# A transformer block in one queue order: a new order of the steps on every engine, and the modulation products in pieces

## The reference

```python
ada = silu(c) @ W_ada + b_ada
shift_msa, scale_msa, gate_msa, shift_mlp, scale_mlp, gate_mlp = split(ada, 6)
h = layernorm(x) * (1 + scale_msa) + shift_msa
x = x + gate_msa * attention(h)          # 16 heads of 18 columns, full softmax
h = layernorm(x) * (1 + scale_mlp) + shift_mlp
x = x + gate_mlp * (gelu(h @ W_fc1 + b_fc1) @ W_fc2 + b_fc2)   # 1152 hidden columns
```

## Time and profile before

| | us |
|---|---|
| three runs | 1205.43, 1207.51, 1208.17 |
| median | 1207.51 |
| the profiled execution's own time | 1206.03 |
| its span, first to last instruction | 1204.2 |
| PE busy | 1161.6 (96%) |
| DVE, ACT, POOL busy | 922.7, 858.0, 578.6 |
| granted TensorE clock, mean of the span | 0.982 |

### The profile page before, as it was taken

The page is one execution under the profiler, slowest core; times in us unless marked ns, Lnnn a source line. Parts: engine busy times, 40 slices in busy tenths (PEclk is TensorE's granted clock), DMA queues, the critical chain, the costliest instruction groups (busy, mean ns, idle before and its releaser), DMA issues.

```text
span 1204.2 us, 28774 instructions
## 1 busy us (share of the span) xinstructions
PE 1161.6 (96%) x10375; PEld 996.8 (83%) x10375; DVE 922.7 (77%) x1928; ACT 858.0 (71%) x1485; POOL 578.6 (48%) x619
## 2 busy tenths in 40 slices
PE   6888999999999999999999999999999999999987
PEld 5656888888888888888888888888888888888777
DVE  5578878878878788787778888877888887877553
ACT  4378777777777777777777787777777777778721
POOL 3012444555544445554454555445455544544664
PEclk9679999999999999999999999999999999999999
DMA  9455554455545445554544555555445555444220
GB/s 283 127 173 159 159 152 154 155 175 172 165 152 174 140 148 173 173 165 156 168 148 150 163 177 169 161 159 165 144 149 177 175 160 158 153 150 161 81 68 20
DMA packets 133815, 186.94 MB, mean 155 GB/s; under 512 B 24284, under 2 KB 102150, under 8 KB 133675
## 3 DMA queue, kind: packets, MB, share of 16 engines
q1 hardware_dynamic: 129193, 175.81, 46.8%
q10 hardware_dynamic: 4482, 9.29, 2.6%
HBM read 119.92 MB, written 64.60 MB: 153 GB/s over the span
## 4 chain that ended last, share of the span: by engine, by line
PE 85%; SPq 5%; DMA 4%; DVE 2%; issue 1%; ACT 1%; POOL 1%; ACTq 0%; POOLq 0%; DVEq 0%
PE a_bank L851 11%; PE x_bank L764 11%; PE turn_bank L818 9%; PE b_bank L851 8%; PE score_bank L789 7%; PE b_bank L865 6%; PE st_bank L806 6%; PE b_bank L866 6%; PE b_bank L867 6%; PE a_bank L832 4%; PE x_bank L772 4%; DMA o_rows<-on 2%; PE x_bank L738 2%; PE a_bank L738 1%; SPq L609 1%
## 5 line engine op out<-in xcount | busy, mean ns | idle before, releaser
L1128 DVE TENSOR_REDUCE mx<-score_bank 128x2 f32<-128x512 f32 x512 | 332.5, 685 | 93.2 <-PE score_bank L789 91.3
L938 ACT ACTIVATE e<-st_bank 128x1024 f32<-128x1024 f32 x256 | 262.6, 1026 | 162.7 <-PE st_bank L806 162.1
L1285 POOL TENSOR_TENSOR gl<-gl_raw,gh 128x512 fp32r<-128x512 f32 (+1 forms) x160 | 197.0, 1239 | 181.2 <-DVE gh L1193 181.2
L931 ACT CAST ql<-mxt 4x256 fp32r<-4x256 f32 x512 | 205.6, 402 | 5.3
L865 PE MATMUL b_bank<-w,gh 128*128 128x288 f32 x576 | 179.2, 311 | 2.0 <-DVE tmp L1199 1.9
L866 PE MATMUL b_bank<-w,gh 128*128 128x288 f32 x576 | 170.7, 296 | 0.0
L867 PE MATMUL b_bank<-w,gl 128*128 128x288 f32 x576 | 169.7, 295 | 0.0
L818 PE MATMUL turn_bank<-e,ve 128*32 128x256 f32 x2048 | 125.5, 386 | 0.4 <-ACT e L938 0.4
L806 PE MATMUL st_bank<-ql,kl 58*128 58x256 f32 x1024 | 118.0, 309 | 6.6 <-ACT e L938 5.9
L789 PE MATMUL score_bank<-kl,ql 58*128 58x256 f32 x1024 | 120.9, 315 | 3.1 <-DVE mx L1128 1.7
L851 PE MATMUL a_bank<-xh,w 128*128 128x256 f32 x640 | 111.7, 297 | 4.3 <-DVE xr L1107 2.8
(11 more groups left out here) (152 smaller groups left out, 2497.6 us busy)
## 6 DMA issues: line engine op xcount, KB each, us to landing
qk_rows<-qst SPq DMA_DIRECT2D x128, 256.0 KB, 3.7
ql<-qk_rows SPq DMA_DIRECT2D x384, 72.0 KB
kl<-qk_rows SPq DMA_DIRECT2D x378, 72.0 KB
o_rows<-on SPq DMA_DIRECT2D x128, 128.0 KB
gate<-gates SPq DMA_DIRECT2D x32, 432.0 KB, 4.6
x<-in_x SPq DMA_DIRECT2D x32, 288.0 KB, 4.1
out<-x SPq DMA_DIRECT2D x32, 288.0 KB, 2.2
xin<-in_x ACTq DMA_DIRECT2D x30, 288.0 KB, 6.4
```

The lines of the kernel that those rows point to most:

```text
L931: last = nc.scalar.copy(rows[:, :, :, a, :], src)
L938: nc.scalar.activation(e[:, j % 4, :, :, :].rearrange("p i u l -> p (i u l)"), st_bank[:, :, :, :].rearrange("p i u l -> p (i u l)"), ACT. ...
L1128: nc.vector.tensor_reduce(mx[:, j // HP, i, :, col:col + 1], score_bank[i][:, :].rearrange("p (t l) -> p t l", t=NT), AX.X, ALU.max).then_ ...
L1285: nc.gpsimd.tensor_tensor(gl[:, cols], g[:, cols], gh[:, cols].bitcast(F32), ALU.subtract).then_inc(g_lo, 1)
```

## The change

All fifteen lists are new; the steps in a period are the same 40 on TensorE, 29 on ScalarE, 45 on VectorE, 17 on GpSimd and 51 on SP. The order of TensorE's period:

```diff
 PE_ORDER = [
-    ("fc2", -3, 0), ("proj", -2, 0), ("st", 0, 1), ("s", 0, 6), ("xt", 2, 0), ("proj", -2, 1), ("st", 0, 2),
-    ("s", 0, 7), ("xt", 2, 1), ("fc2", -3, 1), ("st", 0, 3), ("fc2", -3, 2), ("pv", 0, 0), ("qk", 2, 0),
-    ("fc2", -3, 3), ("s", 1, 0), ("st", 0, 4), ("lt", -2, 0), ("fc2", -3, 4), ("s", 1, 1), ("st", 0, 5),
-    ("lt", -2, 1), ("qk", 2, 1), ("fc2", -3, 5), ("s", 1, 2), ("st", 0, 6), ("fc1", -2, 0), ("s", 1, 3),
-    ("st", 0, 7), ("qk", 2, 2), ("fc1", -2, 1), ("s", 1, 4), ("pv", 0, 1), ("fc1", -2, 2), ("v", 2, 0),
-    ("fc1", -2, 3), ("st", 1, 0), ("s", 1, 5), ("fc1", -2, 4), ("v", 2, 1),
+    ("fc1", -3, 0), ("st", 0, 3), ("s", 1, 0), ("xt", 2, 1), ("fc1", -3, 1), ("pv", 0, 0), ("fc1", -3, 2),
+    ("qk", 2, 0), ("fc1", -3, 3), ("fc1", -3, 4), ("s", 1, 1), ("st", 0, 4), ("qk", 2, 1), ("proj", -2, 0),
+    ("s", 1, 2), ("st", 0, 5), ("fc2", -3, 0), ("proj", -2, 1), ("s", 1, 3), ("st", 0, 6), ("fc2", -3, 1),
+    ("st", 0, 7), ("s", 1, 4), ("fc2", -3, 2), ("qk", 2, 2), ("pv", 0, 1), ("s", 1, 5), ("st", 1, 0), ("lt", -2, 0),
+    ("fc2", -3, 3), ("v", 2, 0), ("st", 1, 1), ("s", 1, 6), ("lt", -2, 1), ("fc2", -3, 4), ("v", 2, 1),
+    ("fc2", -3, 5), ("st", 1, 2), ("s", 1, 7), ("xt", 3, 0),
 ]
```

ScalarE's period, in which the five gelu steps (`fc1`) stand between the exponentials `st` 3 and 4, and `mb(1,0)` behind `st(0,7)`:

```diff
 ACT_ORDER = [
...
-    ("lt", -2, 1), ("st", 0, 5), ("qk", 2, 1), ("st", 0, 6), ("st", 0, 7), ("fc1", -2, 0), ("oh", -1, 0),
-    ("fc1", -2, 1),
+    ("v", 1, 0), ("lt", -3, 1), ("st", 0, 1), ("v", 1, 1), ("oh", -2, 0), ("st", 0, 2), ("xt", 2, 0), ("st", 0, 3),
+    ("fc1", -3, 0), ("xt", 2, 1), ("fetch", 4, 0), ("fc1", -3, 1), ("mb", 0, 1), ("fc1", -3, 2), ("qk", 2, 0),
+    ("oh", -2, 1), ("fc1", -3, 3), ("fc1", -3, 4), ("st", 0, 4), ("pv", 0, 0), ("qk", 2, 1), ("st", 0, 5),
+    ("st", 0, 6), ("st", 0, 7), ("mb", 1, 0), ("qk", 2, 2), ("pv", 0, 1), ("st", 1, 0), ("lt", -2, 0),
 ]
```

TensorE's head, its first lines. It ends with `("st", 3, 2), ("s", 3, 7), ("xt", 5, 0)` where the old one ended with `("fc1", 0, 4), ("st", 3, 0), ("s", 3, 5), ("v", 4, 1)`; the new one has no `fc1`, the new tail has `fc1` of five batches (-5 to -1) where the old one had four:

```diff
 PE_HEAD = [
-    ("xt", 0, 0), ("xt", 0, 1), ("qk", 0, 0), ("qk", 0, 1), ("qk", 0, 2), ("gate2", 0, 0), ("v", 0, 0), ("v", 0, 1),
-    ("xt", 1, 0), ("mod", 0, 0), ("xt", 1, 1), ("gate2", 0, 1), ("s", 0, 0), ("qk", 1, 0), ("s", 0, 1),
-    ("gate5", 0, 0), ("s", 0, 2), ("qk", 1, 1), ("s", 0, 3), ("gate5", 0, 1), ("qk", 1, 2), ("gate5", 0, 2),
+    ("xt", 0, 0), ("xt", 0, 1), ("qk", 0, 0), ("qk", 0, 1), ("qk", 0, 2), ("mod", 0, 0), ("mod", 0, 1), ("v", 0, 0),
+    ("mod", 0, 2), ("v", 0, 1), ("mod", 0, 3), ("xt", 1, 0), ("xt", 1, 1), ("gate5", 0, 0), ("qk", 1, 0),
+    ("s", 0, 0), ("qk", 1, 1), ("s", 0, 1), ("s", 0, 2), ("qk", 1, 2), ("s", 0, 3), ("gate5", 0, 1), ("s", 0, 4),
...
 ]
```

The code, apart from the lists:

```diff
-        w_ada_sb = [e_flat[:, 0:6 * C], e_flat[:, 6 * C:12 * C], gh_raw[0:REM + 1, 0:6 * C]]
         ADA_FIRST = 2 * C
-        c_in, c_exp = x1[0:B, 0, 0, :], x1[0:B, 0, 1, :]
+        w_ada_first = [e_flat[:, 0:ADA_FIRST], e_flat[:, ADA_FIRST:2 * ADA_FIRST], gh_raw[0:REM + 1, 0:ADA_FIRST]]
+        w_ada_rest = [x1[:, :, :, :].rearrange("p a t c -> p (a t c)"),
+                      gate[:, :, :, :].rearrange("p a v c -> p (a v c)")[:, 0:4 * C],
+                      gh_raw[0:REM + 1, ADA_FIRST:6 * C]]
...
+        c_in, c_exp = tmp2[0:B, 0, :], tmp2[0:B, 1, :]
-        sT = rcb[:, 0, 0:3 * B].rearrange("p (k b) -> p k b", k=3)
+        sT = sb("sT", [P, 3, B])[:, :, :]
         mod_of = {0: turn_bank[:, 0:2 * 3 * B],
-                  1: st_bank[:, 0, :, :].rearrange("p u l -> p (u l)")[:, 0:2 * 3 * B]}
+                  1: a_bank[:, C:C + 2 * 3 * B]}
-        gate_val = gate[0:B, 1, :, :]
-        b_fc2_row = e_flat[0:B, 12 * C:13 * C]
+        gate_val = sb("gate_val", [B, 3, C])[:, :, :]
+        b_fc2_row = xn2[0:B, 0, 0:C]
...
+            def gate_store(_b, _n):
+                sp.wait_ge(gates_ready, 3)
+                sp.dma_start(gates_dram, gate_val).then_inc(gates_stored, 16)
+
             def res(b, _):
                 if b == 0:
-                    sp.wait_ge(gates_ready, 3)
-                    sp.dma_start(gates_dram, gate_val).then_inc(gates_stored, 16)
+                    sp.wait_ge(mod_ready, 2)
                     sp.wait_ge(gates_stored, 16)
...
+            def mod_piece(n, i, c, r):
+
+                c0 = MOD_OF[2 * n + i] * C
+                for k, (_r, nr) in enumerate(K_ROWS):
+                    rows = nr + (k == 2)
+                    to = mod_of[n][:, i, c, :] if c < 2 else mod_of[n][REM * r:REM * (r + 1), i, c, :]
+                    last = nc.tensor.matmul(to, w_ada_sb(k, rows, c0 + c * P, min(c0 + (c + 1) * P, c0 + C)),
+                                            sT[0:rows, k, :], start=(k == 0), stop=(k == 2))
+                return last
+
+            MOD_PIECES = [(i, c, r) for i in range(2) for c in range(3) for r in range(1 if c < 2 else 3)]
...
-            def second_mod(_b, _n):
-                pe.wait_ge(ada_rest, 16 * 3)
-                mod_columns(1)
+            def second_mod(_b, n):
+                if n == 0:
+                    pe.wait_ge(ada_rest, 16 * 3)
+                last = mod_piece(1, *MOD_PIECES[n])
+                if n == len(MOD_PIECES) - 1:
+                    last.then_inc(ada_mod, 1)
...
             def st(b, j):
...
-                if b == 0 and j == 0:
-                    pe.wait_ge(gates_ready, 3)
-                    pe.wait_ge(mod_ready, 2)
...
             def proj(b, t):
                 if b == 0:
                     pe.wait_ge(w_split, 6)
+                    pe.wait_ge(gates_ready, 3)
+                    pe.wait_ge(mod_ready, 2)
```

More of the change, by code:

```diff
@@ L83 @@
+    ("om", -2, 1), ("max", 1, 1), ("qk", 2, 0), ("ol", -2, 1), ("max", 1, 2), ("fc1", -3, 1), ("fc1", -3, 2),
+    ("max", 1, 3), ("fc1", -3, 3), ("proj", -2, 0), ("max", 1, 4), ("max", 1, 5), ("fc1", -3, 4), ("qk", 2, 1),
+    ("proj", -2, 1), ("max", 1, 6), ("max", 1, 7), ("mt", 1, 0), ("ln2_stats", -2, 0), ("max", 1, 8), ("max", 1, 9),
+    ("ln2_apply", -2, 0), ("ln2_apply", -2, 1), ("sum2", -3, 0), ("max", 1, 10),
 ]
 POOL_ORDER = [
[3 rows of a table removed]
+    ("clr", 2, 1), ("sum2", -3, 0), ("ln1_stats", 3, 0), ("lt", -2, 0), ("sum2", -3, 1), ("clr", 3, 0),
@@ new lines @@
+    ("qkr", -1, 7), ("qkr", -1, 8), ("qkr", -1, 9), ("or", -4, 4), ("qkr", -1, 10), ("qkw", -1, 4), ("qkr", -1, 11),
+    ("ow", -3, 2), ("ow", -3, 3), ("sw", -3, 0), ("or", -4, 5), ("store", -6, 0), ("rr", -4, 5), ("qkr", -1, 12),
+    ("res", -4, 0), ("rr", -3, 0), ("sw", -3, 1), ("sr", -2, 0), ("qkr", -1, 13), ("qkr", -1, 14), ("qkr", -1, 15),
+    ("ow", -2, 0), ("rr", -3, 1), ("rr", -3, 2), ("qkr", -1, 16), ("rr", -3, 3), ("qkr", -1, 17), ("qkr", -1, 18),
+    ("qkr", -1, 19), ("qkr", -1, 20), ("qkr", -1, 21), ("or", -3, 0), ("or", -3, 1), ("qkr", -1, 22),
[7 rows of a table added]
@@ L270 @@
+    ("or", -1, 5), ("res", -1, 0), ("store", -2, 0), ("store", -1, 0),
 ]
@@ L684, in _ @@
                 load_weights(i)
[L685 removed]
+            run(SYNC_HEAD, SYNC_ORDER, SYNC_TAIL, {"ln1_stats": lambda b, _: None, "gst": gate_store, "res": res, "qkw": qkw, "qkr": qkr, "ow": ow,
                              "sr": sum_read, "sw": rc_write, "rr": rc_read, "or": o_read, "store": store})
@@ L700, in _ @@
             pe.wait_ge(ada_sT, 1)
-            def mod_columns(n):
-                for i in range(2):
-                    c0 = MOD_OF[2 * n + i] * C
-                    for c in range(3):
-                        for k, (_r, nr) in enumerate(K_ROWS):
-                            rows = nr + (k == 2)
-                            for r in range(1 if c < 2 else 3):
-                                to = mod_of[n][:, i, c, :] if c < 2 else mod_of[n][REM * r:REM * (r + 1), i, c, :]
-                                cols = slice(c0 + c * P, min(c0 + (c + 1) * P, c0 + C))
-                                last = nc.tensor.matmul(to, w_ada_sb[k][0:rows, cols], sT[0:rows, k, :],
-                                                        start=(k == 0), stop=(k == 2))
-                last.then_inc(ada_mod, 1)
-            def second_mod(_b, _n):
-                pe.wait_ge(ada_rest, 16 * 3)
-                mod_columns(1)
+            def mod_piece(n, i, c, r):
[7 more added lines that the diff above has]
+            MOD_PIECES = [(i, c, r) for i in range(2) for c in range(3) for r in range(1 if c < 2 else 3)]
+            def mod_columns(n):
+                for i, c, r in MOD_PIECES:
+                    last = mod_piece(n, i, c, r)
+                last.then_inc(ada_mod, 1)
+            def second_mod(_b, n):
[4 more added lines that the diff above has]
+                    last.then_inc(ada_mod, 1)
             def gate_rows(v, k):
@@ L724, in gate_rows @@
                 rows = K_ROWS[k][1] + (k == 2)
-                last = nc.tensor.matmul(gate_of[v][0:B, 0:C], sT[0:rows, k, :], w_ada_sb[k][0:rows, v * C:(v + 1) * C],
+                last = nc.tensor.matmul(gate_of[v][0:B, 0:C], sT[0:rows, k, :], w_ada_sb(k, rows, v * C, (v + 1) * C),
                                         start=(k == 0), stop=(k == 2))
@@ L870, in fc2 @@
                     last.then_inc(b_full, 1)
```

(2 more changed lines are left out.)

155 lines of the change are left out of this document (73 added, 82 removed), and 146 rows, old and new, of tables (ACT_HEAD, ACT_ORDER, ACT_TAIL, DVE_HEAD).

## The result

The changed kernel takes 1200.28 us, median of six runs (1195.84 to 1203.55), the kernel before 1207.49 beside it (1203.65 to 1208.23): a ratio of 0.9949, 95% interval 0.9934 to 0.9964 (the quotient of the two medians is 0.9940, inside it). The forecast was 1194.5, a change of -13 us; the medians say -7.2, the ratio -6.2. The profiled execution took 1197.51 (span 1195.7).

What follows compares the result with a forecast made beforehand. TensorE, busy 1161.6 of 1204.2 us, was taken as the bound. From the profiled 1206.03, -9 (borders), -4 (modulation) and 0 (start and end) gave 1193.0, plus 1.48 to the median: 1194.5 us, range 1187 to 1205.

Steps and rivals of the forecast that it cites:

- Borders: Steady part: fewer switches between full-size and score steps on TensorE shorten the period to 34.5, -9 us over 27 periods.
- rival D: Second step of a couple leaves at 0.43, as one alone, where fc2 or qk follows: 1205.3 us, chance 0.05.
- Steady waits: Steady part: whether the new order brings new waits; cost taken nothing, each 0.1 a period beyond two reserves costing 2.7.
- Both reserves: Steady part: slack of 0.14 from st(0,6) to st(0,7), and 0.24 for st(1,0) behind ScalarE's copies of the maxima.
- Rival C: Slower: copies of mb(1,0) come late and st(1,0) waits 0.79 in every period, 21.3 in all: 1216 us, chance 0.08.
- Modulation: Head: modulation and gate matmuls leave the wait chain ahead of s(0,0); -4 us taken, bounds nothing to 8.3.
- the 38 to 41: Head: predicted start of s(0,0) in us, rather than 43.0, as a sign that the forecast is right.
- Start and end as wholes: Head and tail exchange fc1(0,.) against score steps: head about 6 shorter, tail 5 to 6 longer; net 0, bounds -2 and +2.
- The sum: Whole kernel: -9 - 4 + 0 against the profiled 1206.03 gives 1193.0, with 1.48 for the median 1194.5.
- The coarse count: Steady part: 0.14 per change of array shape, turnings (xt, lt) as full size, 21 to 19 changes: -7.6 in all.

Runs made afterwards that it cites:

- split_couple: Changed kernel with one couple (two score steps in a row) taken apart, st(0,5) moved behind fc2(-3,0): 1209.97 us, ratio 1.0030 to the kernel before.
- mod_whole: Changed kernel with the ten modulation pieces and gate2 together again between xt(1,0) and xt(1,1): 1204.42 us, ratio 0.9975 to the kernel before.
- fill_end: Changed kernel with 36 idle products in the last 25 us of the head, where fc1(0,.) stood: 1203.85 us, ratio 0.9971 to the kernel before.
- again: The changed kernel run once more without any edit: 1200.80 us, median of eight runs, ratio 0.9943 to the kernel before.
- best2: ow_om with 42 idle products in the head, first modulation as changed: 1197.57 us, ratio 0.9930 to the kernel before.
- ow_om2: The kernel of ow_om again, on the same chip as best2: 1201.21 us, ratio 0.9959 to the kernel before.
- turn_off: Changed kernel with lt(0) of a period behind fc2(3) instead of directly behind the couple: 1199.60 us, ratio 0.9943 to the kernel before.
- ow_om: Changed kernel with ow(b,1) directly behind ow(b,0) on SP and lt(0) ahead of om(0) on VectorE: 1198.10 us, ratio 0.9922 to the kernel before.
- warm: Changed kernel with 59 idle products ahead of the head's steps for which TensorE waits: 1198.61 us, ratio 0.9928 to the kernel before.
- best: Changed kernel with the edits of warm and ow_om and the old loop order of the first modulation: 1197.92 us, ratio 0.9929 to the kernel before.
- few_mb: Changed kernel with seven of eight copies of the maxima left out in four half batches of the head: 1201.07 us, ratio 0.9960 to the kernel before.

## Why the forecast was wrong

- **Borders**: right. 34.49 for 34.5, -9.9 us for -9; the second of a couple at 0.33 everywhere (rival D is out), pv into a couple for nothing. split_couple confirms the prices from the other side.
- **Steady waits**, "Cost taken: nothing": 2.0 more than before. Both reserves that the forecast named, 0.14 and 0.24, held. Some 1.4 of the 2.8 hang on a landing: the buffer `on_sb` behind ow(b,1). SP's queue had writes between ow(b,0) and ow(b,1) before too; what the new order changed is that the next copy into `on_sb` comes 12.0 us behind the last instead of 21.5, and the forecast didn't count it. Another 1.2 stand in the first period, where s(4,0) waits for the read of its k rows. Rival C was of this kind, at the wrong place and ten times too large.
- **Modulation**, -4: s(0,0) came 2.3 earlier, at 40.63, inside the 38 to 41, and is held there by its k rows; s(3,0) came 4.8 earlier, and mod_whole loses 3.6. The size is about right. The new loop order, which makes the first modulation 2.3 longer, was overlooked, and is hidden.
- **Start and end as wholes**: this step failed. "So the head gets about 6 shorter and the tail, which must do them, 5 to 6 longer. Net 0, bounds -2 and +2". The tail is 6.1 longer (in five of the later profiles 7.6). The head is 6.2 shorter in all, but 4.8 of that are there at s(3,0) already, ahead of all the exchanged steps. Behind s(3,0), where the 6 us of matmuls left, 1.4 is gained; if one takes the forecast's own 4 for the modulation instead, it is 2.2. So the exchange costs 4 to 5 us and not nothing. The stretch is 24.2 to 26.6 us in the other ten profiles with this order and no idle products in it, with a median of 25.1, so the 25.3 isn't the luck of one profile of the new order; of the old order there is only the one, 26.7. fill_end goes the other way and agrees: 9.0 us of matmuls cost 3.1 there, though at a rising clock; an estimate at that rate is 2.1 for 6.1, and 4 for the exchange. The forecast gave the reason itself ("a head of attention alone leans on ScalarE and VectorE"), and put it at 2 at most. Why 6 us don't come back is shown in its parts: 2.0 more idle time of TensorE, and a lower granted clock for the rest.
- **The sum** then is -9.9 + 2.0 + 6.1 - 6.2 - 0.4 = -8.4, for -8.5 between the profiles. The medians give 1.3 less. That goes with the clock: the profiled run of after had a mean granted clock of 0.985, the median of its six is 0.982. The six go from 1195.84 at 0.985 to 1203.55 at 0.977, the eight of 'again' from 1196.57 at 0.986 to 1205.09 at 0.977; a line through all six falls by 9 us for each 0.01 more of the clock, one through all eight by 6. For 19 runs of the kernel before it falls by 4, and they lie far from it. The kernel before also has the higher clock, 0.985 in the median of these 19 against 0.981 for the eight of 'again': the new order loses some of it. That the clock makes the time, and not something else both, isn't shown; best2 beside ow_om2 points that way.
- The coarse count (one price for each change of shape, -0.28 a period) is 0.09 short of the -0.37 measured. By the Trainium skill, TensorEngine Tiling, Key Properties, what drains TensorE is a change of the tiling mode; the Trainium skill gives no price for it. A turning costs 0.06 more behind a couple than behind fc2 (turn_off), which agrees; but fc2 and v behind a turning pay 0.06 to 0.08, where by that rule they would pay nothing, and there the trace doesn't agree.

Open: why the waits of the first and of the last period come and go between profiles (ow_om 0.1 in all, ow_om2 2.4), and how long the end of the old order's head is in other runs than the one profiled; neither was tried.

## What to carry to other kernels

Work that leaves a stretch and comes back in another is priced at each end by what bounds that end: look for waits and for the granted clock where it leaves, since there only a part of TensorE's time is on the path. When steps are laid out anew, check each buffer that is freed by a landing: how far the next write into it stands behind the last one, and where the write that empties it stands in the DMA queue, not only the engines. And compare profiles by their granted clock before comparing heads: here 0.01 of it goes with 6 to 9 us, as much as the change.

## What the runs showed of the hardware

- TensorE's granted clock falls to the 1.2 GHz level at times in a head in which TensorE rests often (0.79 to 0.89 in the mean of the head), and stays nearer to 2.4 GHz when idle products fill the rests (warm and best2 0.99, best 0.96). The stretches at 1.2 GHz lie elsewhere from run to run; for the same TensorE order of the head it is 137.2 (clock 0.89) to 143.4 (0.86) long, and 149.7 in few_mb (0.79). At 0.89 alone it is 137.2 to 142.4, so the mean clock doesn't say all.
- Matmuls of 32 columns into three different column strips run side by side if they follow one another directly: twelve in 0.36, where four into one strip take 0.35.
- Where st waits for the exponential of the st before, the two stand 1.6 to 1.75 us apart, in few_mb too, with a third less work on ScalarE in that stretch.
- A turning costs 0.06 more behind a couple than behind fc2, and the step behind a turning 0.06 to 0.08 more.
